# One product per half in the mode sums, layer 0's columns on both sides of the last convolution unit, and four images per turn of TensorE's loop

## What is computed

```
x = x + conv(gn(x))       # 3x3 patches without the middle tap, 71 -> 32 -> 8, relu between
x = x + fno(gn(x))
def fno(x):
    h = lift(x, gridx, gridy)                 # 4 groups, 2+2 -> 10 channels each
    for i in range(4):
        h = spectral_conv(h, sp_w1[i], sp_w2[i]) + gconv1x1(h, w_w[i], w_b[i])
        if i < 3: h = gswish(h, betas[i])
    h = gswish(gconv1x1(h, fc1_w, fc1_b), betas[3])    # 10 -> 128 per group
    return gconv1x1(h, fc2_w, fc2_b)                   # 128 -> 2 per group
def spectral_conv(x, w1, w2):
    xf = rfft2(x)                             # 12 low and 12 high rows, 12 columns kept
    out[:12], out[-12:] = complex products of xf with w1, w2, summed over a group's 10 input channels
    return irfft2(out)
```

## Time and profile before

| | us |
|---|---|
| median of three runs | 17488.7 |
| lowest, highest | 17366.53, 17523.27 |
| the profiled execution | 17363.02 |
| its span, first to last instruction | 17361.2 |

### The profile page before, as it was taken

How to read it: one execution, slowest core, us unless ns; L and a number is a source line. 1 busy time by engine, 2 the same in 40 slices (tenths; PEclk the granted TensorE clock), 3 DMA queues, 4 the chain that set the end, 5 groups by cost and what they waited for, 6 DMA issues and landing times.

```text
span 17361.2 us, 558419 instructions
## 1 busy us (share of the span) xinstructions
PE 16419.9 (95%) x246998; PEld 6564.6 (38%) x246998; DVE 6269.9 (36%) x7495; ACT 11026.2 (64%) x10372; POOL 55.3 (0%) x69
## 2 busy tenths in 40 slices
PE   4999999999999999999999999999999999999999
PEld 2334433344433444333443334443344433344333
DVE  4234442234422344323443224442234432344322
ACT  1765567765576655676556676557665567655667
POOL 0000000000000000000000000000000000000000
PEclk9999999999999999999999999999999999999999
DMA  1111111111111111111111111111111111111111
GB/s 44 42 33 44 38 37 45 35 41 38 41 39 42 36 40 38 40 42 33 43 38 38 42 35 43 38 41 39 42 36 41 37 40 43 33 42 38 38 42 34
DMA packets 512312, 681.11 MB, mean 39 GB/s; under 512 B 90930, under 2 KB 483338, under 8 KB 493718
## 3 DMA queue, kind: packets, MB, share of 16 engines
q1 hardware_dynamic: 507318, 642.88, 14.4%
q10 hardware_dynamic: 2408, 0.28, 0.0%
HBM read 507.57 MB, written 135.27 MB: 37 GB/s over the span
## 4 chain that ended last, share of the span: by engine, by line
PE 92%; DVE 4%; issue 2%; DVEq 1%; ACTq 1%; ACT 0%; SPq 0%; DMA 0%
PE PS L702 26%; PE PS L717 24%; PE PS L674 10%; PE PS L666 9%; PE PS L605 7%; PE PS L494 5%; PE PS L555 2%; PE PS L558 2%; PE PS L588 2%; PE PS L504 1%; PE PS L566 1%; PE PS L584 1%; PE PS L527 1%; PE PS L480 1%; PE PS L624 1%
## 5 line engine op out<-in xcount | busy, mean ns | idle before, releaser
L799 ACT ACTIVATE work<-PS 128x512 f32<-128x512 f32 (+1 forms) x8192 | 7939.5, 1021 | 762.9 <-PE PS L702 255.6
L702 PE MATMUL PS<-hmem,fcw 31*128 31x512 f32 x32768 | 4713.9, 645 | 106.9 <-DVE hmem L1109 45.4
L717 PE MATMUL PS<-work,fcw 128*32 128x512 f32 x32768 | 4398.8, 609 | 35.1 <-ACT work L799 33.4
L702 PEld LDWEIGHTS PS<-hmem,fcw 31*128 31x128 f32 x32768 | 1289.0, 184 | 3508.4 <-ACT work L799 3356.5
L792 ACT ACTIVATE hmem<-PS 128x2048 f32<-128x2048 f32 x1056 | 1983.1, 1878 | 663.6 <-PE PS L674 663.6
L1052 DVE STREAM_TRANSPOSE work<-hmem 128x2048 f32<-128x2048 f32 x864 | 1997.3, 2312 | 452.9 <-ACT hmem L792 405.8
L771 ACT ACTIVATE gst<-PS 128x528 f32<-128x528 f32 (+1 forms) x384 | 201.5, 539 | 2782.8 <-PE PS L584 1678.5
L674 PEld LDWEIGHTS PS<-invc,gst 24*128 24x128 f32 x22528 | 1495.7, 330 | 1189.1 <-issue 1188.5
L674 PE MATMUL PS<-invc,gst 24*128 24x256 f32 x22528 | 1917.8, 454 | 0.0
L717 PEld LDWEIGHTS PS<-work,fcw 128*32 128x32 f32 x32768 | 650.9, 108 | 3203.8 <-ACT work L799 3038.3
L1115 DVE SCALAR_TENSOR_TENSOR work<-PS,f2b,work 128x512 f32<-128x512 f32 x224 | 168.2, 751 | 4625.3 <-PE PS L717 4625.3
(11 more groups left out here) (130 smaller groups left out, 9430.4 us busy)
## 6 DMA issues: line engine op xcount, KB each, us to landing
work<-in_x SPq DMA_DIRECT2D x1518, 128.0 KB, 2.5
wspec<-in_spec_w SPq DMA_DIRECT2D x768, 90.0 KB, 2.1
hmem<-x_d SPq DMA_DIRECT2D x128, 528.0 KB
x_d<-work SPq DMA_DIRECT2D x512, 128.0 KB, 2.9
wspec<-in_spec_w SPq DMA_DIRECT2D x768, 60.0 KB, 2.0
fcw<-fcw_d SPq DMA_DIRECT2D x32, 960.0 KB, 5.2
work<-x_d SPq DMA_DIRECT2D x384, 64.0 KB
wspec<-x_d SPq DMA_DIRECT2D x384, 64.0 KB
```

Of the source, the lines that this page charges most:

```text
L702: mm = nc.tensor.matmul(PS[:, fc_bank(p, r), :], f1w[32 * r:32 * r + 31, k, g, :], hmem[32 * r:32 * r + 31, g * PART + u * ROW2:g * PART + ...
L717: mm = nc.tensor.matmul(PS[32 * c:32 * c + 32, 7, :], f2w[:, k, g, :], act[p % 2][:, c * ROW2:c * ROW2 + ROW2], start=kg == 0, stop=final, ...
L799: nc.scalar.activation(act[p % 2][:, strips], PS[:, bank:bank + (3 if rest else 1), :].rearrange("p a b -> p (a b)"), ACT.Silu).then_inc(s ...
```

## The change

It has four parts. In `summed` the second 32 partitions get one product of 120 columns instead of two of 60: the swap of real and imaginary parts is in the output's address pattern (a negative step), the sign is not applied by TensorE any more, and VectorE's move of the result multiplies by a column pair of signs instead of copying. In the body of an image the first half of layer 0's columns (units 0 to 3 of the convolution, as `first_columns(0, b)`) is written around the last `conv2`, two quarter steps before it and two behind, and the second half after all units are turned. Layer 0's `rstd` is applied to the modes before they are multiplied; the additions into `acc` go, and `summed` is called three times per group, for `accl` and the two products, in the place of the filler. The body of the loop is a function `image(i)` and is written four times in a loop of 8 turns. In `pixels` the two loops over strips change places.

```diff
 def turn_columns():
-    pick = np.zeros((4, 32, 2, 4 + 3, 32), np.float32)
+    pick = np.zeros((4, 32, 4 + 3, 32), np.float32)
...
-        PR = 1 + (LAYERS - 1) * WID
+        PR = SC + (LAYERS - 1) * WID
         WSP = 16 * 16
+        TURNS = 4
...
-            with pe.Fori(0, nb) as i:
+            def image(i):
...
+                def first_columns(half, b):
+
+                    for j in (2 * half, 2 * half + 1):
+                        for r in range(4):
+                            mm = nc.tensor.matmul(PS[32 * j:32 * j + 24, r, 0:256], fcol[32 * r:32 * r + 32, 4 * (j % 2) + b, :],
+                                                  turnx[32 * r:32 * r + 32, 8 * half:8 * half + 8, 4 * (j % 2) + b, :],
+                                                  start=b == 0, stop=b == 3, tile_position=(32 * r, 32 * j))
+                    return mm
+
+                pe.wait_ge(s_t0, i * UNITS + UNITS // 2)
+                pe.wait_ge(s_x1, i * UNITS + (UNITS - 1 + HEAD_X1))
+                pe.sem_inc(s_bank, 1)
+                first_columns(0, 0)
+                first_columns(0, 1)
                 conv2(UNITS - 1)
-
+                first_columns(0, 2)
+                first_columns(0, 3)
                 pe.wait_ge(s_t0, i * UNITS + UNITS)
                 pe.sem_inc(s_bank, 1)
-                for b in range(4):
-                    for j in range(4):
...
+                first_columns(1, 0)
+                first_columns(1, 1)
+                group_sum(1, 0, i * 4 + 2)
+                first_columns(1, 2)
+                first_columns(1, 3).then_inc(s_x0, 1)
                 group_sum(1, 1, i * 4 + 2)
...
                     for s in range(2):
                         begin, end = first and s == 0, last and s == 1
                         for t in range(2):
-                            nc.tensor.matmul(to[64 * t:64 * t + 32], sums[:, 0, pick, :], by[:, :, t:WID:2, :, s], start=begin,
-                                             stop=end, tile_position=(0, 64 * t), skip_group_check=True)
-                            for r in range(2):
-                                mm = nc.tensor.matmul(to[64 * t + 32:64 * t + 64, 1 - r], sums[:, r, pick, :],
-                                                      by[:, r, t:WID:2, :, s], start=begin and r == 0, stop=end and r == 1,
-                                                      tile_position=(0, 64 * t + 32), skip_group_check=True)
+                            for back in range(2):
+                                p = 64 * t + 32 * back
+                                to = bass.AP(PS, 4096 * p + 512 * bank + 120 * g + KY * back,
+                                             [[4096, 32], [-KY if back else KY, 2], [2 * KY, 5], [1, KY]])
+                                mm = nc.tensor.matmul(to, sums[:, pick, :], by[:, :, t:WID:2, :, s], start=begin, stop=end,
+                                                      tile_position=(0, p), skip_group_check=True)
...
-                        for r in range(4):
-                            for s in range(4):
+                        for s in range(4):
+                            for r in range(4):
...
-                spin(2, 3)
-                pe.wait_ge(s_pr, i * PR + 1)
                 for g in range(G):
-                    mm = summed(6, g, g, acc, True, True)
-                mm.then_inc(s_sum, 1)
+                    summed(6, g, g, accl, g == 0, False)
+                for n in range(SC):
+                    pe.wait_ge(s_pr, i * PR + (n + 1))
+                    for g in range(G):
+                        mm = summed(6, g, g, prod[n], False, n == SC - 1)
+                    mm.then_inc(s_sum, 1)
...
+            if nb >= TURNS:
+                with pe.Fori(0, nb // TURNS) as j:
+                    for k in range(TURNS):
+                        image(j * TURNS + k)
+            for k in range(nb - nb % TURNS, nb):
+                image(k)
...
+                dve.wait_ge(s_rstd, nth + 1)
+                V.tensor_scalar(spectral_back, spectral_rstd, -1.0, None, ALU.mult)
+                V.tensor_scalar(fs, flat[:, :], spectral_shift, spectral_rstd, ALU.mult, ALU.mult)
...
                 for n in range(SC):
-                    products(prod[n], wl[:, n], fx[:, n, :])
-                dve.wait_ge(s_rstd, nth + 1)
+                    products(prod[n], wl[:, n], fx[:, n, :]).then_inc(s_pr, 1)
...
-                V.scalar_tensor_tensor(acc, prod[0], spectral_rstd, accl, ALU.mult, ALU.add)
-                V.drain()
-                V.scalar_tensor_tensor(acc, prod[1], spectral_rstd, acc, ALU.mult, ALU.add)
-                V.drain().then_inc(s_pr, 1)
...
-                V.tensor_copy(rot[:, :, 0, 0:MODES], PS[:, bank, 0:CH // 2 * MODES].rearrange("p (n m) -> p n m", n=CH // 2))
+                V.tensor_tensor(rot[:, :, 0, 0:MODES].rearrange("p n (r k) -> p n r k", r=2),
+                                PS[:, bank, 0:CH // 2 * MODES].rearrange("p (n r k) -> p n r k", n=CH // 2, r=2),
+                                bass.AP(inside, 7, [[9, 128], [0, CH // 2], [1, 2], [0, KY]]), ALU.mult)
```

57 lines of the change are left out of this document (26 added, 31 removed).

## The result

The changed kernel takes 17153.5 us (median; 17145.3 to 17188.4). The kernel before, timed beside it, takes 17506.0 (17366.5 to 17562.1). The ratio is 0.9858, 95% interval 0.981 to 0.9905: 1.4% faster, clear of no change. The forecast was 17120 in a range of 16970 to 17330. The profiled execution took 17145.3 us against 17363.0, so 218 us less where the sum of the prediction had 320. One execution of each kernel is profiled, and that of the kernel before is faster than all of its timed ones, so what its trace lacks may stand in those. The total came out near the forecast; several of its terms did not, as the table shows.

What follows compares the result with a forecast made beforehand. TensorE, busy 95% of the span, was taken as the bound, with waits and low clock outside the dense layers. Gains 163 + 112 + 45 = 320 us gave 17043 from 17363.0; scaled from 17445, 17120, range 16970 to 17330.

Steps and rivals of the forecast that it cites:

- Mode sums: Layers 1 to 3: fewer instructions shorten each layer's sums from 8.40 to 6.7 us, a gain of 163 us.
- the step behind them: Mode sums: one set of sums follows VectorE's last product, 0.48 us, with the semaphores about 0.55.
- The low clock: Mode sums: the clock is low for a while in part of the layers, TensorE falls behind VectorE, 0.35 us.
- Boundary: Last dense product to first second-convolution product: 24 of 31 lose the branch, 5.0 us instead of 9.67, gain 112 us.
- Layer 0: Path from last second-convolution unit to inverse rows: sums done at 16.4 us instead of 18.3, gain 45 us in all.
- the clock, which I expected "to fall later, not to stay": Layer 0's path: about 4 us of the sums run at half clock and 2.9 at full.
- my rival with a gain of 112: Layer 0: the clock stays up; gain there 112 us, 387 in all, time 17056; chance 0.08.
- A round of sums: Layer 0: each of three rounds takes 1.6 us at full clock and 3.2 at half.
- instructions that arrive late: Layer 0's path: 0.5 us an image taken off the gain of 1.9 us.
- The floor by ScalarE's copy: Layer 0: ScalarE normalises the lifted input, then must copy inverse rows; limits the gain to 3.5 us, 112 us in all.
- Pixels: Mixing products reordered, row strips innermost: taken as no gain, bounds 14 us either way over 1408 units.
- 17445: Starting time midway between lowest and highest runs of the kernel before; times 0.9816 gives 17124, rounded 17120.

## Why the prediction was right, and where it was not

**Mode sums: right mechanism, term too large by 40 us.** The layer at full clock was to take 6.35 us and takes 6.69. VectorE's ten products are 5.78 as worked out (5.8); the step behind them was too small: the move waits 0.91 us, not 0.55. I had taken one set of four out of layer 0's 1.92, but what follows VectorE's last product is, as I read it, a whole set that has yet to start, with its way there and back. The low clock adds 0.43 a layer (7.12 in the mean), where I had 0.35; with one filler product it adds nothing. Of the rule in the Trainium skill, "Runtime: NRT & Kernel Launch", section "Instruction fetch mechanics", that the crossing of a block is mostly hidden: these runs do not agree. 12 products instead of 8, with the same columns, cost 1.03 us a layer, and in layer 3 fetches that came late stopped TensorE for up to 4.9 us. The same section says that a taken branch breaks the prefetch in sequence; the boundary with one image a turn agrees, 307.1 us against 181.3.

**Boundary: right**, 118.6 for 112, since the 80 products overlap better than I took (4.54 us for 5.0). The gap stands at 7 boundaries, and behind the other 24 the clock is never at 1.2 GHz.

**Layer 0: wrong, and near its number on the path by luck.** The path gained 58 us, near the 45, but not by my steps, and only 17.5 of it is lost again when the edit that I had priced is taken out. The step that failed on the path is the clock, which I expected "to fall later, not to stay": it stayed up in 20 of 32 images, which was my rival with a gain of 112. Two terms that I had taken too small worked against it. A round of sums takes 1.9 us at full clock, as before (two take 3.71 in the image above), where I had 1.6, and instructions that arrive late cost 48.4 us, where I had 0.5 us an image, 16 in all. The step that failed behind the path is a term put at nothing without a reason: I ended the sum at the inverse rows and gave the clock no price behind them. It fell there in 11 images, and in pixels it comes back slowly, 17 us an image, which cost 75.5 us in all. Layer 0 as a whole lost 17 us. That the filler goes is not what lets the clock fall, since with the old layer 0 it falls in 13 images. The floor by ScalarE's copy, which I had named as what would make the prediction wrong, shows in a few images only (1.20 us in the one above).

**Pixels: right for a unit** (2.37 us in both orders), but the term had no place for a difference at the low clock, and there the order matters.

**What no step held:** layer 3's stops, -32 us, and the dense layers' clock, +24. Both are matters of where something falls in time; with SyncE's loads where they were, the runs show layer 3 anywhere from 985 to 1096 us.

**The total.** On the scale of the profiled execution the sum gave 17043 us, and 17145 came: 40 us too much in the sums and 108 lost in layers 0 and 3, less 13 from the path, 7 from the boundaries, 24 from the dense layers and 2 of the rest. The forecast of 17120 came nearer because I started from 17445, 82 us above that scale, a start that no row asked for, so its nearness to 17153.5 is luck; the changed kernel's times lie within 43 us of its profiled one, while those of the kernel before spread by 196, and so the ratio of the timed runs (0.9858) and the one of the profiled (17145.3 / 17363.0 = 0.9875) are not the same.

## What to carry to other kernels

Count instructions where small products are chained: at the 14 ns each of the earlier trace rows, eight products of 120 columns beat four of 120 and eight of 60, although the array streams the same. Where TensorE stands still for even 0.7 us ahead of short products, see what the clock does behind that place, not in it: one more filler product here was worth 44 to 77 us behind it in four kernels, for 9 to 24 us ahead of it, and taking all of it away cost 280. Where more small products are put in, look for stops with the releaser issue there too: the three rounds of sums in layer 0 brought 48 us of them. And when a kernel streams long code, look at what the other DMA queues move while the blocks come in; a load that is not needed yet can stop TensorE.

## What the hardware showed that I had not expected

- TensorE, busy for 43.85 of 44.40 us in float32 pixels, stayed at 1.2 GHz; a unit takes 4.00 us there and 2.37 at full clock, so a stop of 1.2 us ahead of it cost about 18.
- A fetch of 16 KB of instructions can come late while other queues are busy. In layer 3 of the kernels with the early loads TensorE stood still for 1.0 to 4.9 us 79 times; the fetch that ended such a stop began 7.8 to 12.3 us after the one before it, where 5.4 to 5.8 us is usual there, while the queues moved 78 to 204 KB per us. With those loads moved by some 30 us, one such stop of 1.16 us was left in 32 images, and none in the kernel with eight images a turn.
- The kernel before showed neither in any of the 32 images of its profiled execution; the one with the edit to the mode sums alone, far from both places, showed the first in 6 images and the second in 9. A profile that is clean at a place does not say that the place is safe.
